# Residual transposed in 32x32 blocks by VectorE and turned by two passes through HBM, with a new order of GpSimd's products

## The reference

```python
# stage 1: one explicit step of a drift-diffusion equation, for each batch
df    = -(grad(A0*f, 1) + grad(A1*f, 2)) + 0.5*(grad2(B0*f, 1) + grad2(B1*f, 2)
        + grad(grad(B2*f, 2), 1) + grad(grad(B2*f, 1), 2))
x     = maximum(f + df*dt, 0)
# stage 2: a conditioned mixture of 8 experts over the 1024 tokens of 128 features
h     = layernorm(x);  h = (h - mean_over_tokens) * rsqrt(var_over_tokens + 1e-8)
gamma, beta = split(small_net(subj_emb[ids]));  gamma = softplus(gamma) + 1e-8
h     = h * gamma + beta
gates = top2(softmax(h @ router_w)), normalised
y     = sum over 8 experts of gate * (relu(h @ w1 + b1) @ w2 + b2)
return x + y
```

## Time and profile before

| | |
|---|---|
| median of 3 runs | 119.1 us (118.77 to 119.17) |
| the profiled execution | 119.23 us, its span 117.4 us |
| TensorE busy | 110.7 us (94% of the span) |
| VectorE busy | 91.3 us (78%) |
| ScalarE busy | 78.5 us (67%) |
| GpSimd busy | 9.9 us (8%) |
| chain that ended last | PE 89%, DVE 6%, ACT 1% |

### The profile page before, as it was taken

How to read it: one execution, slowest core, us unless ns; L and a number is a source line. 1 busy time by engine, 2 the same in 40 slices (tenths; PEclk the granted TensorE clock), 3 DMA queues, 4 the chain that set the end, 5 groups by cost and what they waited for, 6 DMA issues and landing times.

```text
span 117.4 us, 1552 instructions
## 1 busy us (share of the span) xinstructions
PE 110.7 (94%) x512; PEld 86.3 (74%) x512; DVE 91.3 (78%) x199; ACT 78.5 (67%) x110; POOL 9.9 (8%) x20
## 2 busy tenths in 40 slices
PE   6999969999999999999999999999999999999960
PEld 2699757447646788888888888888888888888850
DVE  1475989788992596999949966996799589889781
ACT  0843446785452997777777777777777777777800
POOL 3325930000000000000000000000000000000040
PEclk9999999999999999999999999999999999999999
DMA  2999991000000370040400130040005000400005
GB/s 84 299 395 416 409 395 38 0 0 3 0 0 8 95 265 6 22 156 0 179 0 0 50 131 6 0 144 35 0 0 179 0 0 0 184 0 0 0 0 179
DMA packets 4439, 10.79 MB, mean 92 GB/s; under 512 B 784, under 2 KB 1744, under 8 KB 4432
## 3 DMA queue, kind: packets, MB, share of 16 engines
q1 hardware_dynamic: 3920, 9.93, 23.2%
q10 hardware_dynamic: 512, 0.78, 2.2%
HBM read 10.15 MB, written 0.56 MB: 91 GB/s over the span
## 4 chain that ended last, share of the span: by engine, by line
PE 89%; DVE 6%; ACT 1%; issue 1%; DVEq 0%; ACTq 0%
PE zt L701 11%; PE zt L703 11%; PE zt L702 11%; PE yt L695 6%; PE aux L726 6%; PE aux L729 6%; PE aux L725 6%; PE yt L729 5%; PE yt L726 5%; PE yt L725 5%; PE zt L677 4%; PE zt L561 3%; PE zt L688 2%; PE yt L669 1%; PE yt L584 1%; DVE vs L886 1%
## 5 line engine op out<-in xcount | busy, mean ns | idle before, releaser
L531 ACT ACTIVATE hid_hi<-zt,pv 128x1024 fp32r<-128x1024 f32 x27 | 30.2, 1118 | 17.4 <-PE zt L703 17.2
L1031 DVE TENSOR_TENSOR hid_lo<-hid,hid_hi 128x1024 fp32r<-128x1024 f32 x27 | 33.0, 1220 | 10.0 <-issue 5.4
L536 ACT ACTIVATE hid<-zt,pv 128x1024 f32<-128x1024 f32 x27 | 29.9, 1108 | 0.0
L701 PE MATMUL zt<-h_hi,ws 128*128 128x512 f32 x56 | 22.7, 406 | 0.0
L703 PE MATMUL zt<-h_lo,ws 128*128 128x512 f32 x56 | 21.8, 390 | 0.0
L702 PE MATMUL zt<-h_hi,ws 128*128 128x512 f32 x56 | 21.8, 389 | 0.0
L701 PEld LDWEIGHTS zt<-h_hi,ws 128*128 128x128 f32 x56 | 10.5, 188 | 2.9 <-issue 0.5
L702 PEld LDWEIGHTS zt<-h_hi,ws 128*128 128x128 f32 x56 | 10.5, 188 | 2.5 <-issue 0.5
L703 PEld LDWEIGHTS zt<-h_lo,ws 128*128 128x128 f32 x56 | 10.5, 188 | 2.2
L726 PE MATMUL aux<-hid_hi,ws 128*128 128x512 f32 (+1 forms) x32 | 12.0, 376 | 0.0
L725 PE MATMUL aux<-hid_hi,ws 128*128 128x512 f32 (+1 forms) x32 | 12.0, 376 | 0.0
(11 more groups left out here) (150 smaller groups left out, 149.6 us busy)
## 6 DMA issues: line engine op xcount, KB each, us to landing
we<-in_exp_w_dram SPq DMA_DIRECT2D x8, 512.0 KB, 9.1
gate_all<-gates_dram SPq DMA_DIRECT2D x8, 512.0 KB, 3.6
f<-in_x_dram SPq DMA_DIRECT2D x2, 256.0 KB, 4.6
ft<-in_x_exchanged_dram ACTq DMA_DIRECT2D x2, 256.0 KB, 5.4
out_dram<-acc SPq DMA_DIRECT2D x1, 256.0 KB, 2.1
out_dram<-acc SPq DMA_DIRECT2D x2, 128.0 KB, 2.0
first<-d_difference_dt_ids_dram ACTq DMA_DIRECT2D x1, 136.0 KB, 3.7
gn<-in_grids_dram SPq DMA_DIRECT2D x1, 128.0 KB, 3.8
```

What stands on the lines that cost most here:

```text
L531: act.activation(hid_hi[:, c, :], zt[c % 2][:], ACT.Relu, bias=bias).then_inc(hi_ready, 1)
L536: act.activation(hid[:, c, :], zt[c % 2][:], ACT.Relu, bias=bias).then_inc(hid_ready, 1)
L701: pe.matmul(zt[c % 2][:, tok], w_hi, h_hi[:, tok], start=True, stop=False)
L1031: v.tensor_tensor(hid_lo[:, c, :], hid[:, c, :], hid_hi[:, c, :].bitcast(F32), ALU.subtract).then_inc(lo_ready, 1)
```

## The change

**GpSimd and its partners.** VectorE takes the product `u_a1` of half 1, straight behind its `s_b2`. GpSimd does the other three products of half 1 batch by batch, as twelve instructions of 128x128 instead of three of 128x512: first four of `u_a0` and two of `u_b1`, then it waits for `gamma_ready`, then two of `u_b1` and four of `u_b0`. TensorE's waits follow the batches. The gamma arithmetic moves from GpSimd to VectorE, as two instructions (`gammas`) behind `normalise(0)`; constants change so that half a gamma is no longer formed. ScalarE's `style_log` moves ahead of its `normalise(0)`.

**The residual.** TensorE's eight transposes of `xs` and ScalarE's two copies into `acc` are gone. VectorE transposes each half of `xs` in 32x32 blocks with one instruction of 128x512 (`step_blocks`). SyncE stores the half to an HBM tensor (256 KB), waits for it, and reads it back with four DMAs of 32 partitions, so that the blocks land transposed in `acc`. These transfers stand behind the weights and ahead of the gates in SyncE's list. `add_up(0)` waits for them.

**The start and half 1.** TensorE does 7 matmuls of zeros instead of 8, and `unchanged(1)` moves ahead of the cross terms. Expert 0's first layer on half 1 starts with a whole matmul of 512 columns, after all of `h`.

```diff
-WARM_START = 8
+WARM_START = 7
...
+            for n in range(HALVES):
+                sp.wait_ge(blocks_ready, n + 1)
+                sp.dma_start(step_dram[n], xs_blocks[:, batches(n), :]).then_inc(step_stored, 16)
+                sp.wait_ge(step_stored, 16 * (n + 1))
+                by_feature = step_dram[n].rearrange("(i q) b (j t) -> j q b i t", i=NBLK, j=NBLK)
+                for j in range(NBLK):
+                    to = acc[j * BLK:(j + 1) * BLK, half(n)].rearrange("q (b i t) -> q b i t", b=BH, i=NBLK)
+                    sp.dma_start(to, by_feature[j]).then_inc(acc_in[n], 16)
...
-            pool.wait_ge(s_ready[1], 1)
+            def products(out_, in_, grid, first_batch, count, done):
+
+                for b in range(first_batch, first_batch + count):
+                    pool.tensor_tensor(out_[:, b, :], in_[:, b, :], grid, ALU.mult).then_inc(done, 1)
+
+            pool.wait_ge(a1_ready[1], 1)
+            pool.wait_ge(f_in[1], 16)
+            pool.wait_ge(gn_in, 16)
+            products(u_a0, f, a0_grid, BH, BH, a0_ready[1])
             pool.wait_ge(ft_in[1], 16)
             pool.wait_ge(gt_in, 16)
-            product(u_a1, ft, a1_grid).then_inc(a1_ready[1], 1)
...
+            products(u_b1, ft, b1_grid, BH, 2, b1_ready[1])
             pool.wait_ge(gamma_ready, 1)
-            pool.tensor_scalar(gamma_g[:], half_gamma[:], ln_g, 0.5, ALU.mult, ALU.mult).then_inc(gamma_ready, 1)
+            products(u_b1, ft, b1_grid, BH + 2, 2, b1_ready[1])
+            products(u_b0, f, b0_grid, BH, BH, b0_ready[1])
...
             style_parts()
+            style_log()
             normalise(0)
-            style_log()
+            style_shift()
             inverse_sd_tokens(0)
             conditioned(0)
-            transposed_step(0)
...
             conditioned(1)
-            transposed_step(1)
...
             keep_warm(WARM_START)
             unchanged(0)
+            unchanged(1)
             pe.wait_ge(first_in, 16)
             step_cross(0, 0)
             step_cross(0, 1)
-            unchanged(1)
...
             second_rows_b()
-            step_transposed(0)
...
-            layer1_0_first(0)
-            pe.wait_ge(acc_ready, 1)
+            layer1_0_first()
...
-            step_transposed(1)
             logits(0)
-            layer1_0_first(1)
+            pe.wait_ge(h_ready, sum(H_DVE))
+            pe.wait_ge(h_act_ready, B - sum(H_DVE))
+            layer1_0(1, 0)
             logits(1)
...
+            def step_blocks(n):
+
+                v.transpose(xs_blocks[:, batches(n), :].rearrange("p b j -> p (b j)"),
+                            xs[:, batches(n), :].rearrange("p b j -> p (b j)")).then_inc(blocks_ready, 1)
+
+            def gammas():
+
+                v.wait_ge(glog_ready, 1)
+                v.wait_ge(net_sb, 5)
+                then(v.scalar_tensor_tensor(gsum[:], gpos[:], 1e-8, glog[:], ALU.add, ALU.add))
+                v.tensor_scalar(gamma_g[:], gsum[:], ln_g, 0.25, ALU.mult, ALU.mult).then_inc(gamma_ready, 1)
...
             product(s_b2, f, 1, b2_grid).then_inc(s_ready[1], 1)
+            v.wait_ge(ft_in[1], 16)
+            product(u_a1, ft, 1, a1_grid).then_inc(a1_ready[1], 1)
             feature_stats(0)
             cross_operand(1)
             normalise(0)
+            gammas()
+            step_blocks(0)
+            v.wait_ge(gamma_ready, 1)
             v.wait_ge(gsq_ready, 2)
             token_stats(0)
...
             feature_stats(1)
             normalise(1)
+            step_blocks(1)
             token_stats(1)
...
                     if e == 0:
-                        v.wait_ge(acc_ready, HALVES)
+                        v.wait_ge(acc_in[n], 16 * NBLK)
```

More of the change, by code:

```diff
@@ L28 @@
 BLK = 32
-WARM_START = 8
+NBLK = P // BLK
+WARM_START = 7
 XN_DVE = 2
@@ L74, in batches, with build @@
     return slice(n * BH, (n + 1) * BH)
-def build(nc, gates_dram, first_operands, x, xT, grids, gridsT, second_diff, p128, p64, exp_w, out):
+def build(nc, gates_dram, step_dram, first_operands, x, xT, grids, gridsT, second_diff, p128, p64, exp_w, out):
     with ExitStack() as ctx:
@@ L107, in build @@
         xs = sb("xs", [P, B, P])
+        xs_blocks = sb("xs_blocks", [P, B, P])
         st1 = sb("st1", [P, B, 6])
@@ L127, in build @@
         vs2 = sb("vs2", [P, B])
-        minus_half_g = sb("minus_half_g", [P, 1])
+        minus_quarter_g = sb("minus_quarter_g", [P, 1])
         tg = sb("tg", [P, B])
@@ L154, in build @@
         gsum = sb("gsum", [P, B])
-        half_gamma = sb("half_gamma", [P, B])
         gamma_g = sb("gamma_g", [P, B])
@@ L184, in build @@
         rT = [zt[1][:, half(n)] for n in range(HALVES)]
-        xsT = rT
         small = zt[0][:, half(0)]
@@ L277, in build @@
         h_lo_ready = sem("h_lo_ready")
-        xsT_ready = sem("xsT_ready")
-        acc_ready = sem("acc_ready")
+        blocks_ready = sem("blocks_ready")
+        step_stored = sem("step_stored")
+        acc_in = [sem(f"acc_in{n}") for n in range(HALVES)]
         logits_ready = sem("logits_ready")
@@ L356, in _ @@
             pool.tensor_scalar(onehot[:], idc[:], row_no[:, 0:1], None, ALU.is_equal).then_inc(onehot_ready, 1)
-            def product(out_, in_, grid):
-                return pool.tensor_tensor(out_[:, batches(1), :], in_[:, batches(1), :], over_batches(grid), ALU.mult)
-            pool.wait_ge(s_ready[1], 1)
+            def products(out_, in_, grid, first_batch, count, done):
[5 more added lines that the diff above has]
+            products(u_a0, f, a0_grid, BH, BH, a0_ready[1])
             pool.wait_ge(ft_in[1], 16)
             pool.wait_ge(gt_in, 16)
-            product(u_a1, ft, a1_grid).then_inc(a1_ready[1], 1)
[L366 to L376, removed]
+            products(u_b1, ft, b1_grid, BH, 2, b1_ready[1])
             pool.wait_ge(gamma_ready, 1)
-            pool.tensor_scalar(gamma_g[:], half_gamma[:], ln_g, 0.5, ALU.mult, ALU.mult).then_inc(gamma_ready, 1)
+            products(u_b1, ft, b1_grid, BH + 2, 2, b1_ready[1])
+            products(u_b0, f, b0_grid, BH, BH, b0_ready[1])
             tok = y_last[0][1]
@@ L421, in style_log, with style_shift @@
                 act.activation(glog[:], gexp[:], ACT.Ln, bias=one[:, 0:1]).then_inc(glog_ready, 1)
+            def style_shift():
                 act.activation(beta[:], small[:, B:2 * B], ACT.Identity, bias=pv[:, STY_BB:STY_BB + 1]).then_inc(net_sb, 1)
@@ L473, in conditioned @@
                                    scale=scale[:, b:b + 1]).then_inc(h_act_ready, 1)
-            def transposed_step(n):
-                act.wait_ge(xsT_ready, n + 1)
-                act.activation(acc[:, half(n)], xsT[n], ACT.Copy).then_inc(acc_ready, 1)
             def hidden0(n, c):
@@ L618, in second_rows_a @@
             def second_rows_a():
-                pe.wait_ge(a0_ready[1], 1)
                 for k in range(2):
                     b = BH + 2 * k
+                    pe.wait_ge(a0_ready[1], 2 * k + 2)
                     pe.matmul(pair_of(1, k), neg_diff, u_a0[:, b:b + 2, :].rearrange("p b j -> p (b j)"), start=True,
@@ L632, in second_columns_b @@
             def second_columns_b():
-                pe.wait_ge(b1_ready[1], 1)
                 for b in range(BH, B):
+                    pe.wait_ge(b1_ready[1], b - BH + 1)
                     pe.matmul(own(b), u_b1[:, b, :], half_diff2, start=False, stop=False, skip_group_check=True)
             def second_rows_b():
-                pe.wait_ge(b0_ready[1], 1)
                 for k in range(2):
                     b = BH + 2 * k
+                    pe.wait_ge(b0_ready[1], 2 * k + 2)
                     pe.matmul(pair_of(1, k), half_diff2, u_b0[:, b:b + 2, :].rearrange("p b j -> p (b j)"), start=False,
                               stop=True, skip_group_check=True).then_inc(step_ready, 1)
[L646 to L652, removed]
             def norm_transposed(n):
@@ L677, in layer1_0, with layer1_0_first @@
                 pe.matmul(z0[c], we[:, 0, 0, c, :], h[:, half(n)], start=True, stop=True).then_inc(z0_ready, 1)
[L679 to L683, removed]
+            def layer1_0_first():
+                h_of = h[:, half(0)].rearrange("p (k u j) -> p u k j", k=2, u=2)
                 z_of = z0[0].rearrange("p (k u j) -> p u k j", k=2, u=2)
                 for u in range(2):
-                    pe.wait_ge(h_ready, 2 * n + u + 1)
-                    pe.wait_ge(h_act_ready, 2 * n + u + 1)
+                    pe.wait_ge(h_ready, u + 1)
+                    pe.wait_ge(h_act_ready, u + 1)
                     last = pe.matmul(z_of[:, u], we[:, 0, 0, 0, :], h_of[:, u], start=True, stop=True,
@@ L804, in _ @@
             layer2_0(0, 3)
-            step_transposed(1)
             logits(0)
-            layer1_0_first(1)
+            pe.wait_ge(h_ready, sum(H_DVE))
+            pe.wait_ge(h_act_ready, B - sum(H_DVE))
+            layer1_0(1, 0)
             logits(1)
             for c in range(1, C):
-                if c == C - 1:
```

(13 more changed lines are left out.)

## The result

The changed kernel is slower: 120.68 us median of 6 runs (119.81 to 121.2) against 119.16 of before (118.77 to 119.29), a ratio of 1.0123 with a 95% interval of 1.0091 to 1.0156. Forecast were 118.2 us and a range of 117.5 to 118.9.

A forecast was written before the change was run, and what follows sets the result against it. TensorE bounds the kernel from 36 to 114 us, so only the start counts. Half 0 (-0.15 - 1.15 + 0.35 + 0.2 = -0.75) and half 1 (-0.15) sum to -0.9 us: 118.2 us, range 117.5 to 118.9.

The forecast's parts named there:

- What bounds the kernel now: TensorE, busy 77.42 of 78 us from 36 to 114 us; the change is worth how much earlier it gets there.
- my rivals: Lock moved 0.09, slow transpose 0.05, late gates 0.04, clock level rising later 0.05, more gain than summed 0.14.
- The start: TensorE's start: one matmul of zeros less lets real work begin earlier, worth half of 0.3: -0.15 us (0 to -0.3).
- The wait for GpSimd: Half 0: VectorE's `sq` and `vs` no longer wait for GpSimd's product, 1.03 + 0.12: -1.15 us.
- the small chain beside GpSimd's second products: Half 0: VectorE's small instructions after `token_stats` may wait for GpSimd's last two products: +0.2 us (0 to 0.8).
- the block transpose: Half 0, VectorE: together with the gamma instructions it makes `token_stats` later: +0.35 us (0.1 to 0.9).
- Half 1 and HBM: Half 1: TensorE's first layer starts slightly earlier and needs less time, -0.15 us; the residual's way through HBM delays nothing, 0.

The follow-up runs named there:

- e2: Changed kernel with every SBUF tensor at its old place (blocks declared last, 32 unused bytes for `half_gamma`): 118.95 us, ratio 0.9979.
- e3: Kernel before with every tensor where the changed kernel has it (4,096 unused bytes, `half_gamma` declared last): 120.64 us, ratio 1.0103.
- e15: Changed kernel with 32 unused bytes ahead of `gamma_g`, where `half_gamma` stood, the blocks left in place: 118.93 us, ratio 0.9952.
- e9: Changed kernel at the old SBUF places and with the old start (8 matmuls of zeros, `unchanged(1)` behind the cross terms): 118.93 us, ratio 0.9973.
- e10: Kernel before with the new start alone: 119.63 us, ratio 1.0012.
- e1: Changed kernel again, unaltered: 120.85 us, ratio 1.0116 to the kernel before.
- e12: Kernel before with only `gate_all`, `yg` and `acc` 32 bytes higher: 0.2267 us for a 512-column matmul.
- e4: Changed kernel with the residual as before, through TensorE and ScalarE; tensors from `gamma_g` on 32 bytes lower than before: 120.18 us, ratio 1.0069.
- e11: Changed kernel's GpSimd and VectorE order, with the residual through TensorE as before, old start and old places: 118.84 us, ratio 0.9947.
- e13: Kernel before with 64 unused bytes ahead of the weights' parts and 64 ahead of the hidden tensors: 0.2306 us for a 512-column matmul.
- e18: Kernel before with 128 unused bytes ahead of the weights' parts and 128 ahead of the hidden tensors: 0.2333 us for a 512-column matmul.
- e14: Kernel before with only `hid_lo` 32 bytes higher: 0.2311 us for a 512-column matmul.

## Why the prediction was wrong

**The step that failed** is in "What bounds the kernel now": "nothing on the other engines shortens that stretch as long as it stays fed". I took its length as given and summed only what comes ahead of it. It stayed fed and took 1.65 us longer in the profiled execution, because the pace went from 0.2267 to 0.2322 us. Experiments e2, e3 and e15 show that the places of TensorE's operands in SBUF did this. None of my rivals held it; I had not read the new declaration as an edit of the long stretch.

**The start.** Forecast -0.15; the runs can't tell the term from nothing: e2 and e9 differ by 0.02 us, and e10 is at 1.0012, each with an interval of about 0.3 us either way. In the profile after, TensorE's four matmuls of `unchanged` took 1.03 us, in that of e1 2.04:

```profile
4.45 2.04 PE L585 MATMUL yt<-f,ident 128*128 128x256 f32 x4
...
7.33 1.06 PE L593 MATMUL yt<-u_a,dt_diff 128*128 128x128 f32 x8
...
20.20 1.10 PE L679 MATMUL zt<-h,we 128*128 128x256 f32 x4 [1.10 <-ACT h L479]
```

The same program reached its first row terms (L593) at 5.84 once and at 7.33 once: how long TensorE stays at its lower level differs between executions. The profiles with the old start show 6.10 to 7.54 for it. So the 1.05 us won by 36 us in the first profile are in part luck: its row terms came 0.83 earlier than before, and in e1, the same program, the first layer began at 20.20 in place of 19.00.

**The wait for GpSimd.** The mechanism was right: the two small instructions `sq` and `vs` take 0.16 us each in e1, e2 and e9. In the old order one or both wait, and they end with the product of GpSimd that they meet: in before it is `vs`, in e12 `sq` (14.42 + 0.49 = 14.91, GpSimd's product ends at 14.89). The size, -1.15, fits the execution that the prediction was read from and not every other. From the row terms to the first transpose of `xn` it was 6.67 to 15.79 before; in the profile of e12, whose start is the old kernel's and late, it is 7.54 to 15.83:

```profile
7.54 1.05 PE L593 MATMUL yt<-u_a,dt_diff 128*128 128x128 f32 x8
```

```profile
15.83 0.84 PE L663 MATMUL yt<-ident,xn 128*128 128x128 f32 x4 [0.53 <-DVE xn L895]
```

The old wait ended when GpSimd ended, whatever TensorE's start was, and so it hid a late start. With the new order the interval is 7.96 us in e1, e2, e4 and e9, and a late start goes straight into the result. With the start of the profile before (6.67) it saves 15.79 - 6.67 - 7.96 = 1.16, as summed; with that of e12 (7.54) only 0.33. In after, e11 and e15 the interval is longer, 8.24, 8.22 and 8.94 us, and there something else came last: the DMA of the grid `gt`, for which VectorE's first product waits. In e15:

```profile
7.95 0.69 DVE L841 TENSOR_TENSOR u_b<-ft,gt 128x512 f32<-128x512 f32 x1 [1.95 <-DMA gt<-in_grids_exchanged_dram]
```

```profile
14.78 0.84 PE L656 MATMUL yt<-ident,xn 128*128 128x128 f32 x4 [0.70 <-DVE xn L883]
```

That product started between 6.65 and 8.47 us in the twenty profiles. In the thirteen with the old order the transposes began 8.37 to 8.85 us behind it; in those three of the new order 6.75 to 6.95. So the new order starts them at the later of 7.96 us behind the row terms and about 6.8 behind that product. An estimate from this for each of the thirteen old profiles gives a gain of 0.33 to 1.77 us, 1.0 in the mean; the forecast took the 1.16 of one.

**A gain that no term held.** Of the 107 executions of the experiments with the old order 25 had a mean granted clock under 0.99, and of the 78 with the new order none. In e13, one of the 25, TensorE had just waited 1.34 us for `xn`, and the four microseconds from 16 us on had a granted clock of 0.57 (busy us and instructions of PE, PEld, DVE, ACT, POOL; clock; DMA share; GB/s):

```profile
16.20 1.07 PE L666 MATMUL yt<-ident,xn 128*128 128x128 f32 x4 [1.34 <-DVE xn L898]
```

```profile
16.00:20.00 4.00, 3.81 (x19) 3.72 (x20) 3.14 (x21) 1.78 (x7) 0.67 (x3) 0.57 0.47 183
```

Expert 0's first layer began at 21.44 there, against 19.93 before. With the new order that wait was 0.19 to 0.70 us. That the shorter wait keeps the clock up is likely and not shown: e3 waited 1.96 us at 1.00.

**Blocks and collisions.** From that transpose to the first layer took 4.14 us before, 4.50 in e4 (new order, no block transpose) and 4.91 to 4.93 in after, e1, e2 and e9. Hence the small chain beside GpSimd's second products and the two gamma instructions cost 0.36 (forecast 0.2 for the chain; the gammas hardly count, since `token_stats` starts 0.63 behind the transposes in e4 and 0.60 before), and the block transpose 0.42 (forecast 0.35 with the gammas). Both mis-sized a little, in the foreseen direction.

**Half 1 and HBM.** -0.12 against -0.15, and 0 against 0: right. The first four reads leave at 19.6, when the store behind the weights has landed, the others at 26.96, and the DMA engines are idle from 32 us; I had said 30.

**Sum at equal pace.** With the start of before: -1.16 + 0.36 + 0.42 - 0.12 = -0.5 us. Measured on medians with the pace restored: -0.19 (e2), -0.33 (e9, its own runs of before at 119.26) and -0.46 (e15, before at 119.39). With the mean gain of 1.0 in place of the 1.16 the sum is -0.34, in the middle of these. The forecast of -0.9 was too high by 0.4 to 0.7, for the reasons above; the other 1.9 of the miss is the pace (e1 at 120.85, e2 at 118.95).

**Left open.** Why the distances matter is not shown: no view of the profile has a wait or a conflict in the stretch, only a shorter or longer matmul. What VectorE and ScalarE do at the time is not it: in e18 matmuls during which VectorE ran nothing took 0.2333 us and the others 0.2333, and in the changed kernel it was 0.2332 and 0.2321. Which of TensorE's own operands must agree with which (the moving ones with the weights, or with each other) was not separated; e14 shows that `hid_lo` alone is enough to slow the other layers too (0.2307 for the first layers). Nor was a search made for distances better than those of before.

## What to carry to other kernels

A declaration is an edit: when a change adds, removes or resizes a tensor, everything behind it in SBUF moves, and a stretch that the change does not touch can change its speed by 2.4%, here with whether TensorE's operands begin at the same place modulo 256 bytes. Count the matmuls of a window in both traces before looking for a cause in the edits, and rebuild the kernel before with the new places (and the new one with the old), which costs two runs and tells whether the places are the cause. And a wait on a slow helper also hides the jitter of what runs beside it, so take what its removal is worth from several executions, not from one, and look which input comes last in each.

## What the runs showed of the hardware

Matmuls of 512 columns in fp32r, back to back at a granted clock of 1.00, took 0.2267 us in the ten builds in which all their operands in SBUF begin at the same place modulo 256 bytes, and 0.2306 to 0.2333 us in the nine others. Distances off by 32, 64 or 128 bytes slowed the whole stretch; distances off by 256 or 4,096, and a shift of all tensors together, did not. The slow pace was the same beside an idle VectorE. A VectorE instruction of 128x4 took 1.19 us beside a GpSimd product of 128x512 in place of 0.16 (before), and another 0.50 in place of 0.28 beside products of 128x128 (after). A block transpose of 128x512 fp32 took 0.70 us on VectorE beside GpSimd's products and 0.71 without them, and GpSimd four products of 128x128 in 1.70 us, 0.42 each. Reads of 64 KB in pieces of 128 bytes landed 2.6 us after their issue (median of eight). The mean granted clock was under 0.99 in 25 of 107 executions with the old order of products and in none of 78 with the new.
